# Turning the gathered rows of the edges' targets: from TensorE to VectorE squares and transfers inside SBUF

## What is computed

```
x = swish(x @ lin_W.T + lin_b)
agg1 = segment_sum(f1 * x[src], dst)          # f1, f2: two linear maps of edge features
h1 = swish((agg1 @ rel1.T + b + x @ root1.T) @ lin1.T + b)
agg2, h2: the same with f2
h = concat(h1, h2) @ cat_W.T + cat_b + x
three times: h = swish(h @ lins_i.T + b_i) + h
graph norm over all nodes, final product, layer norm
```

## Time and profile before

| | |
|---|---|
| runs | 5523.48, 5533.62, 5541.32 us |
| span of the profiled execution | 5523.1 us |
| busy | PE 4551.3, DVE 4178.7, POOL 4058.2, ACT 3700.6 us |
| first and last residual activation of the stage (L1259) | start at 2041.0 and 3143.4 us |
| granted TensorE clock, whole core | 0.862 |

### The profile page before, as it was taken

How to read it: one execution, slowest core, us unless ns; L and a number is a source line. 1 busy time by engine, 2 the same in 40 slices (tenths; PEclk the granted TensorE clock), 3 DMA queues, 4 the chain that set the end, 5 groups by cost and what they waited for, 6 DMA issues and landing times. The chain is left out here.

```text
span 5523.1 us, 86293 instructions
## 1 busy us (share of the span) xinstructions
PE 4551.3 (82%) x20518; PEld 2819.0 (51%) x20518; DVE 4178.7 (76%) x8262; ACT 3700.6 (67%) x9029; POOL 4058.2 (73%) x4123
## 2 busy tenths in 40 slices
PE   7999999999999999999999999999677756661000
PEld 4566666666666644444444477777455534451000
DVE  5766666666666658888888899999788854457776
ACT  4777777777777754444444488888688864446665
POOL 6777777777777768777777477777777767777777
PEclk9999999999999999999999999999855555665555
DMA  4556656556565646555555599999799867775443
GB/s 121 142 140 135 136 139 139 139 139 140 139 140 135 140 112 195 178 179 179 176 180 176 170 356 367 365 367 365 270 291 287 276 208 228 230 236 163 134 137 103
DMA packets 558505, 1084.50 MB, mean 196 GB/s; under 512 B 131183, under 2 KB 225065, under 8 KB 558279
## 3 DMA queue, kind: packets, MB, share of 16 engines
q1 hardware_dynamic: 452918, 931.29, 54.7%
q0 software_dynamic: 100352, 149.23, 11.2%
q10 hardware_dynamic: 5008, 1.60, 0.1%
HBM read 648.47 MB, written 438.76 MB: 197 GB/s over the span
## 5 line engine op out<-in xcount | busy, mean ns | idle before, releaser
L832 ACT ACTIVATE p_s<-p_ps,cols 128x512 f32<-128x512 f32 x588 | 404.5, 688 | 317.3 <-PE p_ps L774 207.7
L685 POOL DMA_INDIRECT p_xs<-in_x,src_cols x388 | 376.4, 970 | 221.1 <-DVE p_r L900 131.5
L1163 POOL DMA_INDIRECT ring_rows<-t_rows,home_cols x384 | 446.8, 1164 | 120.4 <-issue 88.6
L692 POOL DMA_INDIRECT home<-edge_row_cols,scatter_cols x392 | 414.8, 1058 | 131.2 <-issue 119.2
L182 POOL DMA_INDIRECT out<-u_res,scatter_cols x392 | 407.2, 1039 | 121.8 <-issue 117.8
L175 POOL DMA_INDIRECT u_rows<-t_rows,home_cols x392 | 388.6, 991 | 145.6 <-issue 118.5
L175 POOL DMA_INDIRECT ring_rows<-t_rows,home_cols x400 | 396.7, 992 | 128.2 <-issue 115.2
L685 POOL DMA_INDIRECT p_xd<-in_x,dst_cols x388 | 391.4, 1009 | 107.5 <-issue 89.0
L1172 POOL DMA_INDIRECT home_cols<-home,src_cols x376 | 379.8, 1010 | 111.4 <-issue 85.9
L1259 ACT ACTIVATE q_s<-q_ps,cols 128x512 f32<-128x512 f32 x294 | 202.1, 687 | 355.9 <-PE q_ps L1236 310.7
L900 DVE TENSOR_TENSOR p_r<-p_s,p_r 128x512 f32<-128x512 f32 x392 | 267.9, 683 | 194.0 <-ACT p_s L832 192.5
(11 more groups left out here) (310 smaller groups left out, 14446.8 us busy)
## 6 DMA issues: line engine op xcount, KB each, us to landing
p_x<-in_x SPq DMA_DIRECT2D x98, 512.0 KB, 6.5
t_rows<-p_o SPq DMA_DIRECT2D x98, 512.0 KB
hT<-ring_own SPq DMA_DIRECT2D x98, 512.0 KB
q_hn<-hT SPq DMA_DIRECT2D x98, 512.0 KB
r_h<-hT SPq DMA_DIRECT2D x98, 512.0 KB
r_x<-t_rows SPq DMA_DIRECT2D x98, 512.0 KB
t_rows<-r_y SPq DMA_DIRECT2D x98, 512.0 KB
t_rows<-r_x SPq DMA_DIRECT2D x98, 512.0 KB
```

The lines of the kernel that those rows point to most:

```text
L685: nc.gpsimd.indirect_dma_start(out=rows[:, j, :], out_offset=None, in_=a["x"], in_offset=bass.IndirectOffsetOnAxis(ap=idx[:, j:j + 1], axi ...
L692: nc.gpsimd.indirect_dma_start(out=tab["home"], out_offset=bass.IndirectOffsetOnAxis(ap=s["scat"][:, k:k + 1], axis=0), in_=s["at"][:, k:k ...
L832: nc.scalar.activation(act_out[i][:, :], flat(bank_r), ACT.Silu, bias=col(LS0 + i)).then_inc(r_act[i], 1)
L1163: nc.gpsimd.indirect_dma_start(out=rows[:, e % 4, j, :], out_offset=None, in_=tab["t1"], in_offset=bass.IndirectOffsetOnAxis(ap=s["home"][ ...
```

## The change

- TensorE no longer transposes the gathered rows, and ACT no longer copies them: L228 and L1266 go, once per step. `bank_t` is left to the single transposition of the home mask in step 5.
- DVE turns block t+3 in step t, by one transpose in 32x32 squares (`turn_squares`, L138), between its last residual addition (`residual(2)`) and the first one (`residual(0)`). In step 0 it turns blocks 0 and 1 at the start and blocks 2 and 3 after the products. The comparison `q_at_home` is done for both halves in step 0.
- SP moves the squares of a pair of blocks to their groups, 16 transfers of 32 partitions x 256 numbers (32 KB each) inside SBUF, in every even step, last in its list for that step (`swap_groups`). It waits for both blocks to be turned.
- PE's `lin` product of block t waits for those 16 transfers and reads `q_xT` through the view `by_column`.
- POOL may gather into a slot when DVE has turned the block in it.

```diff
+def swap_groups(sp, across, turned, sem):
+    for a in range(4):
+        for c in range(4):
+            sp.dma_start(across[32 * c:32 * (c + 1), a], turned[32 * a:32 * (a + 1), c]).then_inc(sem, DMA)
+def by_column(across):
+    return across.rearrange("p a (j i) -> p j a i", j=G)
...
-        xT, xs, xx = sb("q_xT", [P, 2, BLK]), sb("q_xs", [P, 2, BLK]), sb("q_xx", [P, 2, BLK])
+        squares, xT = sb("q_squares", [P, 2, 4, 2, P]), sb("q_xT", [P, 2, 4, 2, P])
+        xs, xx = sb("q_xs", [P, 2, BLK]), sb("q_xx", [P, 2, BLK])
...
+        TURN_AHEAD = 3
...
+                if t % 2 == 0 and live(t, EB):
+                    q = t // 2
+                    sp.wait_ge(squared, t + 2)
+                    after(sp, lined_g, t - 2)
+                    swap_groups(sp, xT[:, q % 2], squares[:, q % 2], xT_in[q % 2])
...
-                        pool.wait_ge(turned, turned_before(e - 4) + 1)
+                        pool.wait_ge(squared, e - 3)
...
-                before = turned_before(t)
-                if t.live(EB):
-                    pe.wait_ge(rows_in[t.of(4)], landed(4, t, G))
-                    after(pe, copied, before)
-                    transpose4(nc, bank_t, rows[:, t.of(4)], s["ident"]).then_inc(turned, 1)
...
-                    pe.wait_ge(copied, before + 1)
+                    q = t.pair()
+                    pe.wait_ge(xT_in[q.of(2)], landed(2, q, 16))
                     after(pe, active_o, t.b)
-                    nc.tensor.matmul(flat(bank_l), s["lin"][:, :], xT[:, t.of(2), :],
+                    nc.tensor.matmul(flat(bank_l), s["lin"][:, :], by_column(xT[:, q.of(2), :, t.slot % 2]),
                                      start=True, stop=True).then_inc(lined_g, 1)
...
-                    act.wait_ge(turned, before + 1)
-                    after(act, lined_g, t.b - 1)
-                    nc.scalar.activation(xT[:, t.of(2), :], flat(bank_t), ACT.Copy).then_inc(copied, 1)
...
+            def turn(e):
+                q = e.pair()
+                dve.wait_ge(rows_in[e.of(4)], landed(4, e, G))
+                if e.past(4):
+                    dve.wait_ge(xT_in[q.of(2)], landed(2, q.back(2), 16))
+                turn_squares(nc, squares[:, q.of(2), :, e.slot % 2].rearrange("p c (j i) -> p c j i", j=G),
+                             rows[:, e.of(4)]).then_inc(squared, 1)
...
                 n = t.back(3)
                 if n.live(EB):
                     residual(2, n)
+                if t.fixed and t.b == 0:
+                    for b in range(2):
+                        turn(t.back(-b))
+                e = t.back(-TURN_AHEAD)
+                if e.past(4) and e.live(EB):
+                    turn(e)
                 n = t.back(2)
                 if n.live(EB):
                     residual(0, n)
```

More of the change, by code:

```diff
@@ L1074, in edges1 @@
         hn_in, nmask_in = ([sem(f"{m}{i}") for i in range(2)] for m in ("hn_in", "nmask_in"))
+        squared, xT_in = sem("squared"), [sem(f"xT_in{i}") for i in range(2)]
         (turned, copied, lined_g, lined_o, active_g, active_o, f_ready, mul1, mul2, scanned1, scanned2, u_done1, u_done2,
@@ L1093, in dense @@
             return [t.back(DENSE_LAG)] if t.back(DENSE_LAG).live(EB) else []
-        def turned_before(t):
-            b = t if isinstance(t, int) else t.b
-            return b + (2 if not isinstance(b, int) or b > MASK_AT else 0)
+        TURN_AHEAD = 3
         idle, paused = sb("q_idle", [P, 8]), sem("paused")
@@ L1112, in _ @@
                 if t == MASK_AT + 2:
-                    sp.wait_ge(copied, MASK_AT + 3)
+                    sp.wait_ge(copied, 2)
                     sp.dma_start(tab["home_mask"].rearrange("o (c q p) -> (o q) c p", q=MC, p=P),
@@ L1245, in step @@
                     for half, chunks in enumerate((range(0, 4), range(4, 7))):
-                        pe.wait_ge(copied, before + 1 + half)
+                        after(pe, copied, half)
                         for c in chunks:
@@ L1293, in step @@
                 if t.fixed and t.b == MASK_AT:
-                    act.wait_ge(turned, before + 2)
+                    act.wait_ge(turned, 1)
                     nc.scalar.activation(mask16[:, 0:4, :], bank_t[0:MC, 0:4, :], ACT.Copy).then_inc(copied, 1)
-                    act.wait_ge(turned, before + 3)
+                    act.wait_ge(turned, 2)
                     nc.scalar.activation(mask16[:, 4:7, :], bank_t[0:MC, 0:3, :], ACT.Copy).then_inc(copied, 1)
@@ L1395, in step @@
                                                    ALU.add, ALU.add).then_inc(r0_ready, 1)
+                if t.fixed and t.b == 0:
+                    for b in range(2, TURN_AHEAD + 1):
+                        turn(t.back(-b))
                 if t.live(EB):
@@ L1408, in step @@
                                                  op0=ALU.mult, op1=ALU.add).then_inc(scanned2, 1)
[L1409 to L1413, removed]
+                if t.fixed and t.b == 0:
+                    for c in range(NC):
+                        dve.wait_ge(home_in[c], DMA)
+                        nc.vector.tensor_tensor(at_home[:, c * CB:(c + 1) * CB, :], home[:, c],
+                                                s["node"][:, c * CB:(c + 1) * CB, :], ALU.is_equal).then_inc(compared, 1)
                 if t.fixed and t.b == 2:
```

## The result

The changed kernel takes 5598.24 us (median of 4 runs, 5595.05 to 5601.44) against 5529.73 us for the kernel before (4 runs): 1.0126 times, 95% interval 1.0112 to 1.0139. The forecast was 5551 us, 5521 to 5598. The direction was right, the size was not: 17 us were forecast and 68.5 came, and the time lies just above the range.

A forecast was written before the change was run, and what follows sets the result against it. The prediction took PE to bound the kernel from step 16 and DVE in steps 8 to 14. Start +22, dense steps +23 and steady steps -28 gave +17 us on the median 5533.62: 5551 us, range 5521 to 5598.

The forecast's parts named there:

- What bounds the kernel: Whole stage: PE bounds from step 16 on, busy 112.00 of 112 us; DVE bounds steps 8 to 14, busy 72.77 of 77.
- The sum: Whole kernel: +22 for the start, +23 for steps 8 to 14, -28 for the steady steps, +17 us in all.
- Part 3, steps 8 to 14: Steps 10, 12 and 14: PE waits 7.6 us each for the 16 transfers, since DVE's masks release SP late; +23 us.
- Part 1, the steady steps: Steps 16 to 97: the step falls from 11.17 to 10.83 us, 0.34 saved in each of 82; 28 us saved.
- a cover of 1.9 us: Steady even steps: slack between the last of 16 transfers landing, 9.9 us after the scan, and PE's need at 11.85.
- (c): All even steps: the 16 transfers come late at 0.60 us an issue; near +65 us, 5599; chance 0.09.
- My circle through both engines: Steady steps: the residual chain through DVE, its new transpose and PE sets the step, 10.87 or 10.78, taken as 10.83 us.
- Part 2, the start: First steps: DVE waits for POOL's gathered rows, needed three steps sooner; 22 us lost, from 12 to 28.
- The two bounds: First steps: late gathered rows, 22 us, and late first transfers behind `ring_home`, 12.4 us, lie beside each other, not added.
- (b): Steady steps: POOL becomes the pace; +45 us, 5579, if it stays at 11.17 a step, 5647 at 12; chance 0.20.
- (d): SP's burst: an issue costs 0.15 us or less, so the kernel gets faster, -24 us, 5510, at best; chance 0.16.
- (e): PE's `lin` product: the change fails to do what it says, for instance `by_column` slows it; 5576; chance 0.05.

The follow-up runs named there:

- e4: Changed kernel with each pair's 16 transfers reading rows of the same size from a DRAM table instead of the squares in SBUF; 5565.11 us, 1.0078.
- e2: Changed kernel with all 16 transfers of a pair issued one step earlier, at the end of SP's list for the step before; 5554.06 us, 1.0048.
- e5: e2 with the first eight blocks turned on PE and copied by ACT, as in the kernel before; 5542.11 us, 1.0023.
- e6: e5 with the product of residual 0 going to `bank_t` from step 8 on; 5541.2 us, 1.0017.
- e3: Changed kernel with the comparison of both halves moved right behind DVE's first two turns; 5598.82 us, 1.0122.
- e10: e2 and e3 together, with DVE's turns two blocks ahead instead of three; 5742.9 us, 1.0385.
- e8: Changed kernel with each transfer, from the third pair on, moving 32 partitions of 256 bytes instead of 1 KB; 5612.25 us, measured once.
- e7: Changed kernel with each transfer, from the third pair on, moving 8 partitions of 1 KB instead of 32; 5609.14 us, measured once.

## Why the prediction was wrong, by its steps

**What bounds the kernel.** Right for PE in the steady steps and DVE in the wide ones.

**The sum.** Forecast 22 for the start, 23 for the wide steps and -28 for the steady ones, 17 in all. Measured 32.5 by step 3, 2.3 from there to step 9, 36.5 in the wide steps and 2.2 behind them, 73.5 in all in the profiled execution.

**Part 3, steps 8 to 14: mechanism right, size off.** Forecast 23, measured 36.5. Even steps 10, 12 and 14 do wait for the transfers, 9.08, 9.83 and 9.83 us for the 7.6 that were forecast; step 8, called in time, waits 1.53. The price of an issue was read from loads out of DRAM (0.45) and is 0.63 to 0.68 for these: about 3 us a burst. At the DRAM price e4 still loses 29.4 us here, so the price is worth 7.1 of the 13.5 us that were missing. For the rest the rows give PE's lower clock behind the wait, 1.9 us in step 10; no run separates it. e2, which takes the burst out of PE's way, brings 36.5 down to 6.4.

The Trainium skill (DMA: Bandwidth & Descriptors, "Issuing engines are not separate DMA queues") says that the time to start a transfer is usually small beside the transfer itself. The trace does not bear this out as a reason to leave it out of a sum: 0.63 to 0.68 us each here, about half of the 1.29 us from the last issue's end to the product that uses it, and PE waits for the last of sixteen.

**Part 1, the steady steps: the step that failed.** Forecast -28, measured +2.2; this is the largest miss. I had given the transfers a cover of 1.9 us at 0.45 an issue. At 0.63 the burst is 9.4 us to its last issue for 6.75, 2.7 longer: the cover is gone and even steps are late, by 0.41 us in the mean. e4 shows that it is the price: at 0.46 they are in time. This is rival (c), given 0.09 with its price of 0.60 written down. With the burst early, e2 measures what the removed transposes are worth: 11.170 - 10.973 = 0.20 us a step, 16 us in all, not 28. The rest lies in two short waits of PE. In e5 its own sum of 10.73 becomes 10.96 by 0.15 for `bank_r`, which the four transposes had covered, and 0.08 for ACT's `q_xx`; without the first a step is 10.93 (e6). My circle through both engines (10.83) left ACT's reading of the bank out.

**Part 2, the start: right in its mechanism, short by the comparison.** Forecast 22, measured 32.5 by step 3. The comparison was put at 0.5 us; it held POOL for 8.88 us and with it the rows, and without that (e3) step 3 is late by 25.4. That POOL "waits for nothing" was true of the kernel before and no longer of this one. The two bounds do lie beside each other, as forecast. The rows alone cost 24.5 us (the growth of step 5 in e5, where nothing else is late). The first transfers alone cost 19.5 (e10), for the 12.4 that were forecast: the first issue behind `ring_home` took 4.21 us and the others 0.63, so the sixteen took 13.71 us for the 7.2 of the forecast. In e3 the larger of the two is left.

**The rivals.** (b), POOL as the pace: POOL has waits in the steady steps of after (for ACT's `q_s`, 37.3 us in all), so no; but its 11.0 us a block is what makes a lead costly, and the versions at 10.93 stand right beside it. (c) is what came, and its 5599 us met the measured 5598.24, but in part by luck: the late even steps cost 0.21 us a step (11.186 for 10.973) where it gave 0.3 to 0.6, and 10.5 us more came at the start, which it did not have. (d) is out, an issue costs more and not less. (e) is out: in e5 and e6 the product behind `lin` stands 0.86 behind it.

## What to carry over

Price a burst of DMA issues by a transfer of the same source and target in the trace, and ask who waits for the last one; then move the burst to where its queue is free before you make it smaller. When data is wanted n steps sooner, find the engine that supplies it: if its pace is nearly that of the step, the lead is paid once, nearly in full wherever it is begun (24.5 us at step 5, 17.1 at step 13). An instruction removed from the bounding engine is worth its time only if no short wait lies under it.

## What the runs showed of the hardware

An issue on SP's queue of an SBUF-to-SBUF transfer takes 0.63 us in line (16 in 10.03), the same for 32 partitions of 1 KB (e2), 32 of 256 bytes (e8) and a little more for 8 of 1 KB (0.67, e7). One from DRAM with 32 partitions of 1 KB takes 0.46 (e4), close to the 0.45 of the loads from DRAM in the earlier trace rows. PE's granted clock was 0.50 of full speed from 2174.5 to 2184.0, in the last 5 us of a wait of 9.08 us and behind it, and its products then stood up to 1.87 us apart for 0.86; over steps 9 to 14, with three such waits, it was 0.85 in the mean.
